# Where ScalarE computes the two magnitudes of a window: the order of ScalarE's instructions in 179 windows of a fused SSM, MLP and FP4 feed-forward kernel

## The chip, the cores and the metric

The kernel runs on one core of a Trainium2 chip. The metric is the device time of one execution in microseconds. The kernel before took 3205.65 us (median of three runs, 3205.09 to 3207.87).

## The reference

The input x is 2 x 4096 tokens of 512 features, in float32. It is layer-normalised to xn, and the output is `x + attn(xn) + ffn(xn)`. The attention branch is a state-space layer and a GELU MLP of width 2048. The feed-forward branch is a gated layer of width 1408 whose operands are all rounded to FP4 in blocks of 16. It is this branch that the change touches:

```python
def fp4_quant_dequant(x):                      # blocks of 16 along the last dim
    xb = x.reshape(shape[:-1] + (shape[-1] // 16, 16))
    scale = max(max|xb| / 6, 1e-12)
    idx = searchsorted(_MID, abs(xb / scale))  # the nearest of 0 .5 1 1.5 2 3 4 6
    return _GRID[idx] * sign(xb) * scale
def fp4_linear(x, w):
    return einsum('bsk,nk->bsn', fp4_quant_dequant(x), fp4_quant_dequant(w))
gate, y = fp4_linear(xn, w_gate), fp4_linear(xn, w_up)
ffn = fp4_linear(silu(gate) * y, w_down)

x1  = xn + ssm_scan(rmsnorm(xn, scale1), A, B, C, D)
attn = x1 + gelu(rmsnorm(x1, scale2) @ w1 + b1) @ w2 + b2
```

## The kernel before

Five engines run programs that are written out by hand and meet at semaphores. After a head (up to 116 us) come 179 windows, numbered by `s`. After them, from 1784 us, the MLP of the attention branch runs alone.

A window works on 256 to 512 tokens and one of 11 slices of 128 hidden features. `h(w)` is the gated product of window w. TensorE computes in window s the gate half and the up half of slice s (L747), and multiplies h(s-2) with the down weights (L769). Each product is done in three passes of a high and a low part, so 12 matmuls each of the three.

All other engines turn h(s-1) into FP4 in that window. In the order of the data:

- ScalarE computes silu(s) from the gate bank into `sg`, L1319. There is one buffer `sg`, so silu(s) also waits until VectorE has taken h(s-1) out of it (L960). TensorE can't begin the gate half of s+1 before silu(s) has read the bank.
- VectorE multiplies (L952), transposes within blocks (L960), and finds the scales (L987, L998, L992). This group is called the front.
- GpSimd divides by the scales, L1518 (`scaled`).
- ScalarE takes absolute values times a constant, L1284 (`magnitude`), into PSUM bank 4, or into `qb` from window 96 on.
- VectorE rounds with two instructions (L1004, L1012), GpSimd multiplies the scales back (L1524, `dequant`), VectorE transposes back (L966).
- In the next window ScalarE rounds to the high part (L1312, `h_high`), and GpSimd subtracts to get the low part (L1532, `h_low`). In GpSimd's program h_low(s-1) stands ahead of scaled(h(s)).

Many windows have a side job as well: in windows 1, 2, 3, 4 and 6 a piece of a weight, in 60 others a tile of 128 tokens of x, to be brought to FP4 in the same way. A side job of window s gets its front and its L1518 at the end of window s, and its rounding in s+1. A weight is then turned by TensorE (L717), split into a high part by ScalarE (L1290, `high`) and a low part by VectorE (L1019, `low`). That is in window s+3, and VectorE's `low` stands ahead of its L960. A tile of x goes out to DRAM and comes back transposed (L508, L516). VectorE takes it up in window s+3 (L1027), and ScalarE makes its high part (L1294).

Further work shares the windows. In windows 11 to 62 it is the SSM's kernel: in 32 windows ScalarE computes two `taps` (an Exp and a Copy each, L1339 and L1347), and two windows after every second of these `kernel_v` (L1355). Exp and Silu have different tables, so each change between them has a table load. In windows 66 to 97 ScalarE writes two tiles of the SSM's input each (`uwrite`, L1371). SyncE sends them to DRAM (L446) four at a time. In windows 99 to 162 the SSM itself runs. ScalarE copies inputs (L1381) in one window and results (L1389) in the next. TensorE has extra matmuls (L793, L810, L818), and VectorE a scan (L1107). Before it can begin, all SSM inputs must be in DRAM: in window 97 GpSimd waits for that (L1589), and SyncE does before it issues the first loads.

In the trace ScalarE's, VectorE's and GpSimd's instructions stand in the order of their programs. So what a `window` function lists first is waited for first. The change touches ScalarE's `window`. On ScalarE `h_job(s)` is h(s-1), `side(s)` the side job of window s.

## Time and profile before

| | |
|---|---|
| three runs | 3205.09, 3205.65, 3207.87 us |
| the profiled execution | 3205.09 us, of which the span of the profile is 3203.3 us |
| TensorE | busy 3081.2 us (96%), granted clock 0.995 |
| VectorE | 2005.0 us (63%) |
| ScalarE | 1090.4 us (34%) |
| GpSimd | 1149.7 us (36%) |
| the chain that ended last | TensorE 60%, VectorE 19%, issue 8%, GpSimd 6%, ScalarE 4% |

A busy share says what an engine does, not what ends last. Matmuls follow each other in a pipeline and their ends are modelled, so TensorE counts as busy where it is near its peak and also where it is a little behind. The pace of the windows shows it better: silu(11) starts at 210.2 us, silu(63) at 661.6, silu(97) at 949.4, silu(103) at 1018.4 and silu(163) at 1652.1.

### The profile page before, as it was taken

How to read it: one execution, taken by the hardware profiler on the slowest of the kernel's cores; microseconds unless marked ns; L12 is line 12 of the kernel's file. 1: busy time of each engine (PE TensorE's matmuls, PEld its weight loads, DVE VectorE, ACT ScalarE, POOL GpSimd, SP SyncE). 2: the span in 40 equal slices, each digit the busy share in tenths (PEclk: the TensorE clock that was granted, in tenths of full speed). 3: DMA queues.
4: the chain of work that ended last, by engine and by line, in shares of the span. 5: the costliest groups of instructions: out<-in, count | busy, mean ns of one | idle time of the engine just before them, and what ended most of it. 6: DMA issues, size and time to landing. Idle time of an engine off the chain costs nothing.

```text
span 3203.3 us, 43122 instructions
## 1 busy us (share of the span) xinstructions
PE 3081.2 (96%) x14861; PEld 2475.4 (77%) x14861; DVE 2005.0 (63%) x4427; ACT 1090.4 (34%) x1910; POOL 1149.7 (36%) x1097
## 2 busy tenths in 40 slices
PE   5789999999998999999999999999999999999999
PEld 3578777777876777777777788888888888888887
DVE  7788888877776666666677654444445444444442
ACT  5435656645443333433332321121222111212121
POOL 7555666655554554554554211010111111111100
PEclk9999999999999999999999999999999999999999
DMA  4133334346765666566643433333333333333320
GB/s 118 47 86 93 109 116 120 85 133 169 188 176 140 161 166 163 143 159 159 159 117 96 124 74 73 73 76 63 79 73 78 68 72 72 73 71 72 74 56 17
DMA packets 865577, 335.58 MB, mean 105 GB/s; under 512 B 680400, under 2 KB 771792, under 8 KB 862800
## 3 DMA queue, kind: packets, MB, share of 16 engines
q1 hardware_dynamic: 865360, 332.83, 42.6%
q8 instruction: 119, 1.95, 0.3%
q14 instruction: 98, 0.80, 0.1%
HBM read 225.21 MB, written 107.51 MB: 104 GB/s over the span
## 4 chain that ended last, share of the span: by engine, by line
PE 60%; DVE 19%; issue 8%; POOL 6%; ACT 4%; SPq 2%; DMA 2%; DVEq 0%; ACTq 0%; POOLq 0%
PE bank L885 22%; PE bank L869 22%; PE bank L747 8%; PE bank L769 4%; POOL qa L1524 3%; DVE qs L987 3%; DVE qa L1004 3%; DVE qa L960 2%; DVE sg L952 2%; DVE qb L1012 2%; POOL qa L1518 2%; PE bank L810 2%; ACT ub L1371 1%; DVE qs L998 1%; DVE qb L966 1%
## 5 line engine op out<-in xcount | busy, mean ns | idle before, releaser
L869 PE MATMUL bank<-hT,Wp 128*128 128x512 f32 x3072 | 745.2, 391 | 4.6 <-ACT gf L1469 2.5
L885 PE MATMUL bank<-Wp,G 128*128 128x512 f32 x3072 | 743.8, 391 | 0.0
L869 PEld LDWEIGHTS bank<-hT,Wp 128*128 128x128 f32 x3072 | 577.7, 188 | 130.7 <-ACT gf L1469 2.9
L885 PEld LDWEIGHTS bank<-Wp,G 128*128 128x128 f32 x3072 | 576.7, 188 | 126.0
L747 PE MATMUL bank<-XT,Wu 128*128 128x512 f32 (+1 forms) x2148 | 520.5, 391 | 28.6 <-DVE sg L952 27.6
L747 PE MATMUL bank<-XT,Wg 128*128 128x512 f32 (+1 forms) x2148 | 525.1, 394 | 18.9 <-DVE Wd L1019 10.2
L769 PE MATMUL bank<-Wd,HT 128*128 128x512 f32 x2112 | 515.0, 392 | 0.5 <-POOL HT L1532 0.3
L747 PEld LDWEIGHTS bank<-XT,Wu 128*128 128x128 f32 x2148 | 397.4, 190 | 132.6 <-issue 53.3
L1218 DVE CAST G<-gf 128x512 fp32r<-128x512 f32 x256 | 110.3, 431 | 610.6 <-PE bank L885 590.1
L747 PEld LDWEIGHTS bank<-XT,Wg 128*128 128x128 f32 x2148 | 398.6, 190 | 108.5 <-issue 15.8
L769 PEld LDWEIGHTS bank<-Wd,HT 128*128 128x128 f32 x2112 | 394.3, 188 | 95.6 <-issue 14.2
L1524 POOL TENSOR_TENSOR qa<-qb,qs 128x512 f32<-128x512 f32 (+2 forms) x277 | 308.0, 1112 | 375.2 <-DVE qb L1012 372.8
L1469 ACT ACTIVATE gf<-bank,vec 128x512 f32<-128x512 f32 x256 | 176.1, 688 | 614.5 <-PE bank L869 614.5
L1518 POOL TENSOR_TENSOR qa<-qa,qs 128x512 f32<-128x512 f32 (+1 forms) x243 | 263.2, 1083 | 225.2 <-DVE qs L992 225.2
L1607 POOL TENSOR_TENSOR zx<-zl,b2r 128x512 f32<-128x512 f32 x64 | 87.0, 1360 | 618.8 <-DMA out_dram<-zx 533.7
L1532 POOL TENSOR_TENSOR HT<-qb,HT 128x512 fp32r<-128x512 f32 (+1 forms) x179 | 230.1, 1286 | 139.3 <-ACT HT L1312 139.2
L1610 POOL TENSOR_TENSOR zx<-zx,xl 128x512 f32<-128x512 f32 x64 | 82.8, 1294 | 515.8 <-DVE xl L1178 515.7
L1312 ACT ACTIVATE HT<-qb 128x512 fp32r<-128x512 f32 (+1 forms) x179 | 112.2, 627 | 351.4 <-DVE qb L966 351.4
L966 DVE STREAM_TRANSPOSE qb<-qa 128x512 f32<-128x512 f32 (+1 forms) x179 | 122.0, 682 | 131.4 <-POOL qa L1524 131.4
L1220 DVE TENSOR_TENSOR G<-gf,G 128x512 fp32r<-128x512 f32 x256 | 185.9, 726 | 8.8
L1319 ACT ACTIVATE sg<-bank 128x512 f32<-128x512 f32 (+1 forms) x179 | 105.8, 591 | 218.4 <-PE bank L747 187.1
L1004 DVE SCALAR_TENSOR_TENSOR qa<-qb,qa 128x512 f32<-128x512 f32 (+2 forms) x149 | 113.2, 760 | 98.4 <-ACT qb L1284 97.9
(114 smaller groups left out, 2840.2 us busy)
## 6 DMA issues: line engine op xcount, KB each, us to landing
px<-in_L_attn_x_dram SPq DMA_DIRECT2D x128, 256.0 KB, 3.2
xin<-in_L_attn_x_dram SPq DMA_DIRECT2D x128, 256.0 KB, 3.5
sT<-r_K SPq DMA_DIRECT2D x128, 256.0 KB, 4.2
r_Z<-xin SPq DMA_DIRECT2D x64, 256.0 KB, 2.2
r_U<-ub SPq DMA_DIRECT2D x16, 1024.0 KB, 6.6
sU<-r_U SPq DMA_DIRECT2D x32, 512.0 KB, 5.2
r_Y<-sY SPq DMA_DIRECT2D x16, 1024.0 KB, 5.7
xl<-in_L_attn_x_dram SPq DMA_DIRECT2D x64, 256.0 KB, 3.1
```

The lines of the kernel that those rows point to most:

```text
L747: ins = e.matmul(bk[:, 0:n], W[wh][:, k, :], inputs(xh, w, k), start=(k == 0 and p_ == 0), stop=(k == KD - 1 and p_ == 2))
L769: ins = e.matmul(DNB[t % 4][:], HT[hh][:, w % 2, a * P:(a + 1) * P], Wd[wh][:, f, :], start=(w == first(n) and p_ == 0), stop=(w == last(n ...
L869: ins = e.matmul(bk[:], Wp[f][wh][:, 0, k * P:(k + 1) * P], hT[xh][b % 2][:, k, :], start=(k == 0 and p_ == 0), stop=(k == KD - 1 and p_ = ...
L885: ins = e.matmul(ACC[j][:], G2[gh][:, n % 2, j * P:(j + 1) * P], Wp[f][wh][:, 1, :], start=(f == 0 and p_ == 0), stop=(f == 15 and p_ == 2))
L966: e.transpose(qb[:, m % 2, 0:n], qa[:, m % 4, 0:n]).then_inc(s_t2, 1)
L1004: e.scalar_tensor_tensor(Aa, Bb, FLOOR, Aa, ALU.max, ALU.add).then_inc(s_t, 1)
L1220: e.tensor_tensor(G2[1][:, n % 2], gf[:, n % 2], G2[0][:, n % 2].bitcast(F32), ALU.subtract).then_inc(s_glo, 1)
L1312: e.activation(HT[0][:, w % 2, 0:n], qb[:, m % 2, 0:n], ACT.Copy).then_inc(s_hh, 1)
L1469: e.activation(gf[:, n % 2], PB[n % 2][:], ACT.Gelu, bias=vec[:, f:f + 1]).then_inc(s_gl, 1)
L1518: e.tensor_tensor(blk(qa[:, m % 4, 0:n]), blk(job_in(m)), bc(qs[:, m % 4, 1, 0:n // 16], n // 16), ALU.mult).then_inc(s_pa, 1)
L1524: e.tensor_tensor(blk(qa[:, m % 4, 0:n]), blk(qb[:, m % 2, 0:n]), bc(qs[:, m % 4, 0, 0:n // 16], n // 16), ALU.mult).then_inc(s_ph, 1)
L1532: e.tensor_tensor(lo, qb[:, m % 2, 0:n], hi.bitcast(F32), ALU.subtract).then_inc(s_hl, 1)
```

## The change

The order of the calls in ScalarE's `window` changes. Nothing is computed in another way, and no other engine's program changes.

- The magnitude of h(s-1) moves from behind silu(s), kernel_v and the uwrites to ahead of silu(s).
- The magnitude of a side job moves from the middle of window s+1 to the end of window s. In the row of ScalarE's instructions it now stands ahead of the next window's `high`, `h_high` and `x_high`, where it was behind them.
- The uwrites move behind the taps; with the magnitude ahead of silu they are also behind that. `kernel_heads` moves ahead of `kernel_v`.

```diff
                 if side(s - 3) in XPOS:
                     x_high(side(s - 3))
-                if side(s - 1) is not None:
-                    magnitude(side(s - 1))
+                if h_job(s) is not None:
+                    magnitude(h_job(s))
                 if s < NW:
                     silu(s)
+                if s in (K0 - 3, K0 - 2):
+                    kernel_heads(s - K0 + 3)
                 if s - 2 in TAPS[1::2]:
                     kernel_v(TAPS.index(s - 2) // 2)
-                for n in plan_slice(s):
-                    if LATER[n][0] == "uw":
-                        uwrite(LATER[n][1])
-                if h_job(s) is not None:
-                    magnitude(h_job(s))
-                if s in (K0 - 3, K0 - 2):
-                    kernel_heads(s - K0 + 3)
                 j = tap_pair(s)
                 if j is not None:
                     kernel_taps(j)
                     kernel_taps(j + 1)
+                for n in plan_slice(s):
+                    if LATER[n][0] == "uw":
+                        uwrite(LATER[n][1])
                 if k == -1:
                     ssm_inputs(0)
                 if 0 <= k < 2 * NV - 2 and k % 2 == 0:
                     ssm_inputs(k // 2 + 1)
+                if side(s) is not None:
+                    magnitude(side(s))
                 if 0 <= k < 2 * NV and k % 2:
                     ssm_result(k // 2)
```

The first place is ScalarE in windows 4 and 5, early in the run, where side jobs are weights. `Wd0<-bank0` is `high`, `HT0<-qb` is `h_high`, `qb<-qa` is the magnitude of the side job and `bank4<-qa` that of h. Before:

```order
L1290 ACTIVATE Wd0<-bank0 128x4x128
L1312 ACTIVATE HT0<-qb 128x256
L1284 ACTIVATE qb<-qa 128x384
L1319 ACTIVATE sg<-bank0 128x512
L1284 ACTIVATE bank4<-qa 128x512
L1290 ACTIVATE Wd0<-bank0 128x3x128
L1312 ACTIVATE HT0<-qb 128x512
```

The same place in the changed kernel:

```order
L1290 ACTIVATE Wd0<-bank0 128x4x128
L1312 ACTIVATE HT0<-qb 128x256
L1284 ACTIVATE bank4<-qa 128x512
L1319 ACTIVATE sg<-bank0 128x512
L1284 ACTIVATE qb<-qa 128x384
L1290 ACTIVATE Wd0<-bank0 128x3x128
L1312 ACTIVATE HT0<-qb 128x512
```

The two magnitudes have changed places around silu. In the second piece the one into `qb` belongs to the next side job, and `high` and `h_high` now stand behind it.

The second place is ScalarE in windows 97 and 98, where the last uwrites are (`ub<-px`). From here the magnitude of h goes into `qb` too. `sUc<-sU` is the first copy of SSM inputs. Before:

```order
L1319 ACTIVATE sg<-bank0 128x512
L1371 ACTIVATE ub<-px,nb,rst 128x32x8 x4
L1284 ACTIVATE qb<-qa 128x512
L1312 ACTIVATE HT0<-qb 128x512
L1284 ACTIVATE qb<-qa 128x512
L1319 ACTIVATE sg<-bank0 128x512
L1284 ACTIVATE qb<-qa 128x512
L1381 ACTIVATE sUc<-sU 128x64x16
```

And in the changed kernel:

```order
L1284 ACTIVATE qb<-qa 128x512
L1319 ACTIVATE sg<-bank0 128x512
L1371 ACTIVATE ub<-px,nb,rst 128x32x8 x4
L1284 ACTIVATE qb<-qa 128x512
L1312 ACTIVATE HT0<-qb 128x512
L1284 ACTIVATE qb<-qa 128x512
L1319 ACTIVATE sg<-bank0 128x512
L1381 ACTIVATE sUc<-sU 128x64x16
```

The four ACTIVATEs of the last uwrites have moved behind the magnitude of h(96) and behind silu(97). The magnitude of side job 97 stands ahead of h_high(96).

## Rows read from the trace of the kernel before

**Rows 1.** Windows view: length; PE, PEld, DVE, ACT, POOL busy; TensorE's clock; DMA; GB/s.

```profile
210.20:661.60 451.40, 440.07 (x1933) 353.39 (x1932) 377.01 (x761) 261.24 (x401) 271.81 (x279) 1.00 0.36 105
...
949.40:1018.40 69.00, 60.71 (x343) 47.04 (x342) 45.92 (x85) 24.84 (x33) 34.35 (x33) 0.95 0.56 136
1018.40:1652.10 633.70, 617.17 (x4081) 482.73 (x4081) 422.77 (x896) 241.60 (x314) 319.25 (x305) 0.99 0.61 157
```

**Rows 2.** Waits of the whole run: us in total, times, longest us.

```profile
DVE qa L1004 <- ACT qb L1284: 97.9, 61, 4.9
```

**Rows 3.** Timeline, windows 79 and 80: start, length, engine and line, idle before.

```profile
798.96 1.06 POOL L1518 TENSOR_TENSOR qa<-qa,qs 128x512 f32<-128x512 f32 x1 [0.76 <-DVE qs L992]
...
800.12 0.58 ACT L1284 ACTIVATE bank<-qa 128x512 f32<-128x512 f32 x1
...
804.02 1.07 POOL L1518 TENSOR_TENSOR qa<-qa,qs 128x512 f32<-128x512 f32 x1 [0.50 <-DVE qs L992]
...
804.55 0.63 ACT L1312 ACTIVATE HT<-qb 128x512 fp32r<-128x512 f32 x1 [3.85 <-DVE qb L966]
...
805.26 1.30 POOL L1532 TENSOR_TENSOR HT<-qb,HT 128x512 fp32r<-128x512 f32 x1 [0.17 <-ACT HT L1312]
...
807.31 1.38 POOL L1518 TENSOR_TENSOR qa<-qa,qs 128x512 f32<-128x512 f32 x1 [0.76 <-DVE qs L992]
```

**Rows 4.** Timeline, window 5 (the weights).

```profile
142.83 0.49 ACT L1290 ACTIVATE Wd<-bank 128x384 fp32r<-128x384 f32 x1 [1.96 <-PE bank L717]
...
145.12 0.84 POOL L1518 TENSOR_TENSOR qa<-xin,qs 128x384 f32<-128x384 f32 x1
...
145.75 0.54 DVE L1019 TENSOR_TENSOR Wd<-bank,Wd 128x384 fp32r<-128x384 f32 x1
...
145.99 0.52 ACT L1284 ACTIVATE qb<-qa 128x384 f32<-128x384 f32 x1
```

**Rows 5.** Timeline, window 9.

```profile
188.90 1.06 POOL L1518 TENSOR_TENSOR qa<-qa,qs 128x512 f32<-128x512 f32 x1 [1.03 <-DVE qs L992]
...
192.50 0.69 DVE L1004 SCALAR_TENSOR_TENSOR qa<-bank,qa 128x512 f32<-128x512 f32 x1 [1.26 <-ACT bank L1284]
```

**Rows 6.** Timeline, window 22 (a table load ahead of silu).

```profile
306.86 1.28 ACT L1319 ACT_TABLE_LOAD   x1
...
308.15 0.60 ACT L1319 ACTIVATE sg<-bank 128x512 f32<-128x512 f32 x1
308.17 1.06 POOL L1518 TENSOR_TENSOR qa<-qa,qs 128x512 f32<-128x512 f32 x1 [1.15 <-DVE qs L992]
...
311.47 3.02 PE L747 MATMUL bank<-XT,Wg 128*128 128x512 f32 x12
```

**Rows 7.** Timeline, windows 97 to 99 (the SSM begins).

```profile
949.90 2.07 ACT L1371 ACTIVATE ub<-px,nb,rst 128x256 f32<-128x256 f32 x4
...
951.99 0.38 SPq L446 DMA_DIRECT2D r_U<-ub  x1
952.13 0.63 ACT L1284 ACTIVATE qb<-qa 128x512 f32<-128x512 f32 x1 [0.16 <-POOL qa L1518]
...
958.38 0.31 POOL L1589 MEMSET sB<- 128x256 f32 x1 [1.95 <-DMA r_U<-ub]
...
976.42 0.71 DVE L1027 STREAM_TRANSPOSE XW<-xin 128x512 f32<-128x512 f32 x1 [8.11 <-DMA xin<-r_X]
...
978.56 4.51 PE L747 MATMUL bank<-XT,Wg 128*128 128x512 f32 x12 [3.81 <-ACT sg L1319]
...
980.22 0.63 ACT L1284 ACTIVATE qb<-qa 128x512 f32<-128x512 f32 x1 [1.80 <-POOL qa L1518]
...
984.91 4.58 PE L747 MATMUL bank<-XT,Wu 128*128 128x512 f32 x12 [1.84 <-DVE sg L952]
```

**Rows 8.** Timeline, windows 126 to 128 (the SSM).

```profile
1262.51 0.32 SPq L508 DMA_DIRECT2D r_X<-qa  x1
...
1285.72 1.98 PE L810 MATMUL bank<-sT,sUc 128*64 128x128 f32 x16 [4.77 <-DVE sS L1107]
```

## The prediction

> **What bounds the kernel now.** I read the windows view first, by stages. In the reader's terms a stage is limited by TensorE where its idle time is near nothing. From 1784 us on that is so, and the change doesn't reach there. In the SSM's stage (windows 103 to 162) TensorE is idle for 633.70 - 617.17 = 16.5 us only; elsewhere it is the bound [rows 1]. In windows 11 to 62 it counts as idle for 451.40 - 440.07 = 11.3 us, and VectorE is busy for 377 of 451 us [rows 1]. There, and in the windows before 11, the timeline shows a ring that no engine can shorten alone: VectorE's product of h, front, GpSimd's L1518, ScalarE's magnitude, VectorE's rounding, GpSimd's L1524, VectorE's transpose back, and then the next product.
>
> Next I read who waits for whom. VectorE waits 97.9 us in 61 cases for the magnitude in `qb` [rows 2]. That looks like the prize of this change. But a wait for an instruction doesn't say that this one was held up by its neighbours. So I compared, window by window, when the magnitude of h starts with when its input is ready. In window 79 GpSimd's L1518 ends at 798.96 + 1.06 = 800.02 and the magnitude starts at 800.12, although the uwrites stand ahead of it [rows 3]. In windows 11 to 97 it is like this nearly everywhere. The wait is the time that GpSimd and ScalarE need. In the SSM's stage the magnitude does stand behind a silu that waits for TensorE's gate half, by 0.4 to 1.4 us, but there TensorE is the bound and VectorE has time.
>
> **What the change costs and gives, stage by stage.** The instructions are the same ones, as many, and as many table loads; only waits move. The h magnitude gets a free way. The price is with what now stands behind a magnitude: in windows after a side job these are `high`, `h_high`, `x_high`, and everywhere silu and the uwrites.
>
> *Windows 1 to 10.* In window s+3 of a weight, VectorE's `low` (L1019) stands ahead of its L960 and waits for ScalarE's `high`. Before, `high` ran as soon as TensorE had turned the weight, at 142.83 for window 5, long before `low` at 145.75 [rows 4]. Now the next side job's magnitude stands ahead of it, and its input is ready at 145.12 + 0.84 = 145.96. So: magnitude until 146.0 + 0.52 = 146.5, `high` until 147.0, `low` at 147.1 instead of 145.75. That is 1.35 us, and it is on the ring: L960, front and everything after move with it. It happens five times, in windows 4, 5, 6, 7 and 9, since the window before each has a side job: 5 x 1.35 = 6.8 us. In three further windows `h_high` alone is late, 0.4 us each by the working of the next paragraph: 1.2 us. Against it stands a gain. In window 9 L1518 ends at 189.96, but VectorE gets the magnitude only for 192.50, after a wait of 1.26 us [rows 5], since silu(9) waits for TensorE. Now it doesn't: -1.2 us, and -0.4 us in two like windows. Together **+6.4 us**. Bounds: +1 if `low` gets room that I don't see (VectorE idle before it; no row shows any), +9 if each is a full magnitude and `high` later than now and nothing is gained.
>
> *Windows 11 to 96.* In window 80 `h_high` ran at 804.55, and `h_low` at 805.26 to 806.56, ahead of L1518 at 807.31 on the same engine [rows 3]. Side job 79's input for its magnitude is ready at 804.02 + 1.07 = 805.09. Now the magnitude comes first, until 805.7, `h_high` until 806.4, `h_low` from 806.4 to 807.7, L1518 at 807.7: 0.4 us late, and the ring with it. Of 13 side jobs in windows 63 to 96, seven lie like this one. At the others VectorE has a tile of x to take up first and hides it. That gives 2.8 us. Of 18 in windows 11 to 62 about eight are not hidden, at 0.4 each, 3.2 us; where there are taps too `h_high` is up to 0.9 us late for L1518, but VectorE has statistics to do there. Gains: the magnitude starts 0.05 us sooner without uwrites ahead of it (some 25 windows), 1.1 us sooner once in window 95, and 0.2 us in four windows with kernel_v: -3 us. Together **+3 us**, with -3 (no `h_high` matters) and +8 (none is hidden) as bounds.
>
> Silu is later as well. In window 22 it ran at 308.15 after its table load; now it must follow L1518 (ends at 309.23), magnitude, load and silu, 0.6 + 1.28 + 0.6, and is over at 311.8. TensorE's next gate half began at 311.47 [rows 6], so it is 0.4 us late, in some ten windows. I cost this at nothing: the up half behind it waits for VectorE's product anyway. If that cover were gone it would be 4 us.
>
> The Trainium skill (ScalarE: Activation LUTs, "What ACT_TABLE_LOAD costs") gives a change of table 1283 ns and a drain of about 1380 ns behind it. The load of 1.28 us is as the page says; the drain is not in this trace, where silu starts at 308.15 and the load ended at 308.14 [rows 6]. By the page silu would be over another 1.4 us later than I have it, and rival 3 is the case that would come of it.
>
> *Windows 97 to 102, where the SSM begins.* The last four ACTIVATEs of the uwrites started at 949.90 and ended at 951.97; the DMA to DRAM was issued at 951.99; and GpSimd could go on at 958.38 after waiting for it [rows 7]. SyncE's first SSM loads wait for the same DMA, and behind them in its queue stands the way back of tile 96, for which VectorE waits 8.11 us until 976.42. Now the uwrites stand behind the magnitude, which can't start before 952.13 and takes 0.63, and behind silu: they start at 953.3, 3.4 us later, and the chain to 976.42 moves with them. A second piece follows. TensorE waited for silu(99) until 978.56. Silu(99) now stands behind a magnitude that starts at 980.22, so it is over at 981.4, and the gate half starts 2.9 us later. It takes 4.51 us at the lower clock, to 986.0; the up half had begun at 984.91, after an idle 1.84. Of the 2.9 us thus 1.1 are left. From here TensorE is the bound. Together 3.4 + 1.1 = **+4.5 us**. Bounds: +1 (the loads hide part of the DMA) and +3.4 + 2.9 = +6.3.
>
> *Windows 103 to 162.* TensorE loses its 16.5 us in eight stalls, the longest 4.77 [rows 1, 8]. They come from tiles of x whose way back is late. The way out is issued when the tile is rounded, as at 1262.51 [rows 8], and VectorE gets there a little earlier now. But SyncE's SSM loads stand in between, and they wait for TensorE's results. I take 0.5 us for each of seven: **-3.5 us**, between 0 and -16.5. In windows where a side magnitude now stands ahead of the copy of results, the copy is about 0.5 us later; it isn't needed before TensorE's next SSM states, most of a window later.
>
> The sum is 6.4 + 3 + 4.5 - 3.5 = +10.4 us. The profiled execution took 3205.09 us, 1.8 more than its span, and stands 0.6 below the median of the runs. So the time is **3215.5 us**, 0.3% slower than before.
>
> **Rivals.**
> 1. *Nothing that can be measured*, 3207 us. Half of the +9.4 us before window 97 is hidden by idle time of VectorE that I don't see, and of the start of the SSM only the 3.4 us stay: 4.7 + 3.4 - 3.5 = 4.6, and another 3 us come back from the stalls in the SSM's stage. For it speaks that VectorE is busy for 377 of 451 us, so it isn't always the one waited for. Against it: the ring waits for one after the other, and idle time of one engine is the work of the next.
> 2. *Faster*, 3197 us. The place is the SSM's stage. If the free magnitude lets each tile of x leave early enough, the eight stalls go, 16.5 us, and with them TensorE's time at the lower clock: the mean of 0.99 [rows 1] over 617 us is some 6 us. That is -22 against +13.9 for the rest. For it: the 97.9 us of waits are mostly in this stage [rows 2]. Against it: it decides from the point at which a tile leaves as much earlier as TensorE's stall lasts, up to 4.8 us, and the magnitude gives 1.4 at most.
> 3. *Much slower*, 3232 us. Silu behind the magnitude holds up TensorE's gate half for so long that the up half and VectorE's next product wait too. The case needs silu to stay away after its table load for about as long again as the load lasts, 1.28 us. Then the gate half is 0.4 + 1.28 = 1.7 us late in some ten windows, 17 us, for TensorE has little room in this stretch. It decides from about 1 us of lateness, the time between the gate half's end and the product that the up half waits for. For it: window 22 has no room left. Against it: the trace shows silu right behind the load [rows 6]. It is what the Trainium skill's rule on the drain would lead to.
>
> **How the numbers follow.** My forecast has a chance of 0.60 (its own range is 3210 to 3224), rival 1 0.23, rival 2 0.09, rival 3 0.08. A difference of 0.2%, 6.4 us, is about what a measurement of this kernel can tell from none. Faster by more than that is rival 2: 0.09. Slower is rival 3 and nine tenths of the forecast, 0.62; the rest, 0.29, is no change. The range that should hold the time 8 times in 10 goes from 3201 (into the ground between rivals 1 and 2) to 3228 us, short of rival 3.
>
> **What would show it.** In window 5 of the changed kernel `low` waits for ScalarE's `high`, by about 1.3 us, where it waited for nothing. In side windows GpSimd's L1532 ends where L1518 begins, without a gap. The DMA r_U<-ub of window 97 is issued about 3.4 us later, after allowing for the shift so far, and the first gate half of the SSM's stage again waits for silu. VectorE's wait for L1284 in the SSM's stage gets shorter and TensorE's stalls hardly do. If silu(11) comes no later than 212 us, the first term is wrong; if silu(103) isn't at least 8 us later than 1018.4, the second and third are; if the stretch from there to silu(163) is shorter by more than 8 us, I misjudged the stalls.

## The result, and the profile after

The changed kernel takes 3249.96 us (median, 3246.31 to 3250.7), the kernel before 3206.76 in the same comparison: ratio 1.0132, interval 1.0114 to 1.0149. The profiled execution of it took 3252.47 us, with a span of 3250.7. The prediction was 3215.5 with a range of 3201 to 3228. The direction was right, and the size was wrong by a factor of four.

Where the time went is best seen by the start of VectorE's L960, which comes once a window. What each stretch takes more than in the kernel before, in us, with the kernels of the experiments below:

| kernel | 1 to 10 | 10 to 62 | 62 to 97 | 97 to 103 | 103 to 163 | 163 to 179 |
|---|---|---|---|---|---|---|
| predicted | +6.4 | +2.4 | +0.4 | +4.5 | -3.5 | 0 |
| changed kernel | +7.4 | +15.0 | +20.6 | +2.9 | -0.9 | +1.7 |
| e1 uwrites first | +7.7 | +15.1 | +6.0 | -1.5 | -0.5 | +1.7 |
| e2 side magnitude in the middle | -0.6 | +3.6 | +12.5 | +1.0 | -0.3 | +1.9 |
| e3 both | -0.7 | +3.6 | -1.8 | -1.7 | -3.5 | +1.9 |
| e4 side magnitude alone | +11.6 | +13.4 | +8.5 | -0.2 | +8.8 | +0.8 |
| e5 uwrites alone | 0.0 | -0.1 | -1.4 | -3.2 | +1.4 | -0.1 |
| e6 scales in PSUM, 66 to 96 | +5.4 | +15.2 | +16.2 | +2.4 | -3.4 | +1.7 |
| e7 `high` first | +0.6 | +15.4 | +18.5 | +2.2 | +1.0 | +1.8 |
| e8 tile out first | +7.5 | +15.3 | +8.4 | +2.7 | -4.5 | +1.8 |
| e9 h first from 64 on | +2.0 | +0.5 | -1.3 | -3.3 | -2.4 | +2.0 |
| e11 scales in PSUM, to 95 | +8.2 | +5.0 | +16.6 | +1.7 | -2.5 | +1.7 |
| e10b e9 with scales in PSUM | +1.9 | -0.5 | +1.4 | -3.4 | -3.0 | +2.0 |

(The prediction's +3 for windows 11 to 96 is 3.2 - 0.8 for its first part, with the gains at kernel_v, and 2.8 - 2.4 for its second.) e5 and e9 have the same program up to window 63 and differ by 2.0 in the first stretch and 0.6 in the second. e7 has the changed kernel's program from window 10 on and differs from it by 0.3 in windows 10 to 62, 2.0 in 62 to 97 (nearly all in window 94) and 1.9 in the SSM's stage, where the five kernels with the changed order (the changed one, e1, e6, e7, e11) lie from -3.4 to +1.0. So fine, and no finer, is what one profile of each tells.

The windows view of the changed kernel, over the windows of [rows 1] (length; PE, PEld, DVE, ACT, POOL busy; clock; DMA; GB/s):

```profile
220.40:687.60 467.20, 442.14 (x1929) 354.91 (x1928) 393.40 (x760) 256.84 (x401) 274.51 (x281) 1.00 0.35 102
996.40:1064.40 68.00, 56.62 (x327) 43.59 (x326) 42.57 (x80) 24.17 (x34) 32.44 (x31) 0.95 0.56 139
1064.40:1699.05 634.65, 617.68 (x4080) 482.95 (x4079) 417.06 (x897) 244.76 (x314) 321.74 (x306) 0.99 0.60 157
```

Windows 11 to 62 are 15.8 us longer, and in them VectorE is busy for 393.40 us instead of 377.01, though it has the same work. Instructions that take longer without doing more are held up inside themselves. That was the first trace of what I had missed. The page of the changed kernel (chain by engine; groups: busy, mean ns, idle before) shows the rest:

```profile
PE 56%; DVE 20%; POOL 8%; issue 8%; ACT 3%; DMA 3%; SPq 2%; DVEq 0%; POOLq 0%; ACTq 0%
...
L1532 POOL TENSOR_TENSOR HT<-qb,HT 128x512 fp32r<-128x512 f32 (+1 forms) x179 | 230.2, 1286 | 241.9 <-ACT HT L1312 241.9
...
L1004 DVE SCALAR_TENSOR_TENSOR qa<-qb,qa 128x512 f32<-128x512 f32 (+2 forms) x149 | 107.2, 719 | 98.6 <-ACT qb L1284 98.4
```

VectorE's wait for the magnitude in `qb`, 97.9 us before [rows 2], is 98.4 us now: the magnitudes came earlier in the program and not earlier for the one who waits. GpSimd's wait for `h_high` went from 139.2 us on the page of before to 241.9.

**Windows 3 to 9.** Window 5 as in [rows 4] (start, length, engine and line, idle before):

```profile
147.24 0.52 ACT L1284 ACTIVATE qb<-qa 128x384 f32<-128x384 f32 x1 [4.02 <-POOL qa L1518]
147.67 0.47 ACT L1290 ACTIVATE Wd<-bank 128x384 fp32r<-128x384 f32 x1
148.04 0.62 ACT L1312 ACTIVATE HT<-qb 128x512 fp32r<-128x512 f32 x1
148.18 0.56 DVE L1019 TENSOR_TENSOR Wd<-bank,Wd 128x384 fp32r<-128x384 f32 x1 [1.10 <-ACT Wd L1290]
148.65 0.70 DVE L960 STREAM_TRANSPOSE qa<-sg 128x512 f32<-128x512 f32 x1
```

Magnitude, `high`, `low`, L960, each on the heels of the one before. `low` waits 1.10 us here and 6.2 us in its five cases. It waited for nothing before.

**Window 80, a side window of x.** Against [rows 3], in the changed kernel:

```profile
834.90 1.06 POOL L1518 TENSOR_TENSOR qa<-qa,qs 128x512 f32<-128x512 f32 x1 [0.51 <-DVE qs L992]
...
836.00 0.63 ACT L1284 ACTIVATE qb<-qa 128x512 f32<-128x512 f32 x1 [1.94 <-POOL qa L1518]
836.07 0.71 DVE L960 STREAM_TRANSPOSE qa<-sg 128x512 f32<-128x512 f32 x1
...
836.53 0.62 ACT L1312 ACTIVATE HT<-qb 128x512 fp32r<-128x512 f32 x1
...
837.23 1.28 POOL L1532 TENSOR_TENSOR HT<-qb,HT 128x512 fp32r<-128x512 f32 x1 [1.26 <-ACT HT L1312]
837.54 1.00 DVE L998 TENSOR_SCALAR qs<-qs 128x32 f32<-128x32 f32 x1
...
839.01 1.38 POOL L1518 TENSOR_TENSOR qa<-qa,qs 128x512 f32<-128x512 f32 x1 [0.51 <-DVE qs L992]
```

The kernel before, VectorE in the same window:

```profile
805.20 0.71 DVE L960 STREAM_TRANSPOSE qa<-sg 128x512 f32<-128x512 f32 x1
...
806.66 0.18 DVE L998 TENSOR_SCALAR qs<-qs 128x32 f32<-128x32 f32 x1
```

ScalarE and GpSimd do what I had worked out: magnitude, `h_high`, `h_low`. But L998, a scaling of 32 columns that took 0.18 us, now takes 1.00 us. It starts at 837.54, while GpSimd's L1532 runs (837.23 to 838.51), and ends at 838.54, when that one is over. From L960 to L1518 it is 839.01 - 836.07 = 2.94 us instead of 807.31 - 805.20 = 2.11: 0.83 us, and the releaser of L1518 is still VectorE's L992 and not L1532. Before, L1532 had ended at 806.56, 0.1 us ahead of L998. Of the window steps (L960 to L960) 7 in windows 11 to 62, 7 in 63 to 96 and 7 in the SSM's stage are longer by 0.80 to 0.84 us, about this number each time.

It is the same wherever L998 is long. All 67 cases over 0.26 us in the changed kernel, and all 38 in the kernel before, end 0.03 to 0.04 us after the end of a GpSimd instruction that ran beside them, L1532 in nearly every case.

**Windows 63 to 97: the late tiles.** Side tile 86 in the changed kernel. (L1371 is the uwrite, L1524 the tile's dequant, L446 the DMA of uwrites, L508 and L516 the tile's way out and back, L1027 its taking up.)

```profile
901.75 2.07 ACT L1371 ACTIVATE ub<-px,nb,rst 128x256 f32<-128x256 f32 x4
```

```profile
901.33 1.07 POOL L1524 TENSOR_TENSOR qa<-qb,qs 128x512 f32<-128x512 f32 x1 [0.63 <-DVE qb L1012]
```

```profile
903.84 0.38 SPq L446 DMA_DIRECT2D r_U<-ub  x1
904.26 4.35 SPq L508 DMA_DIRECT2D r_X<-qa  x1
...
912.29 2.60 SPq L516 DMA_DIRECT2D xin<-r_X  x4
```

```profile
916.65 0.71 DVE L1027 STREAM_TRANSPOSE XW<-xin 128x512 f32<-128x512 f32 x1 [3.18 <-DMA xin<-r_X]
```

The same in the kernel before, SyncE and then VectorE:

```profile
867.34 0.38 SPq L446 DMA_DIRECT2D r_U<-ub  x1
869.16 2.88 SPq L508 DMA_DIRECT2D r_X<-qa  x1
...
875.00 2.60 SPq L516 DMA_DIRECT2D xin<-r_X  x4
...
880.18 0.69 DVE L1027 STREAM_TRANSPOSE XW<-xin 128x512 f32<-128x512 f32 x1
```

The tile was ready at 902.40, when L1524 ended. SyncE stood at L446, which waits for uwrites that end at 903.82; the tile left at 904.26, 1.86 us late. Before, it left 0.02 us after its dequant, at 869.16. It then goes out 0.42 us behind the DMA of uwrites, and I take it that the two share the DMA engines: 8.03 us from the way out to the way back, instead of 5.84. Together 4 us, and VectorE, which had not waited for this tile, waits 3.18. The next such tiles wait 3.17 (0 before) and 4.25 (0.71 before). The steps that answer to them, from windows 88, 92 and 94 to the next, are longer by 3.23, 3.24 and 3.51.

**Windows 97 to 99**, against [rows 7]:

```profile
996.85 2.06 ACT L1371 ACTIVATE ub<-px,nb,rst 128x256 f32<-128x256 f32 x4
...
998.94 0.38 SPq L446 DMA_DIRECT2D r_U<-ub  x1
...
1005.71 0.31 POOL L1589 MEMSET sB<- 128x256 f32 x1 [5.56 <-DMA r_U<-ub]
...
1022.91 0.71 DVE L1027 STREAM_TRANSPOSE XW<-xin 128x512 f32<-128x512 f32 x1 [6.68 <-DMA xin<-r_X]
...
1027.97 3.00 PE L747 MATMUL bank<-XT,Wg 128*128 128x512 f32 x12 [3.38 <-ACT sg L1319]
...
1031.40 2.97 PE L747 MATMUL bank<-XT,Wu 128*128 128x512 f32 x12 [0.43 <-DVE sg L952]
```

L960 of window 97 is at 948.60 before and at 991.47 now. From there the DMA of uwrites is 4.1 us later than before, the tile 3.6 and the gate half 6.5. But the up half is only 3.6 later, since the gate half takes 3.00 us and not 4.51. The windows view of the two gate halves, before and changed, has the reason in its clock column:

```profile
978.50:983.10 4.60, 4.51 (x12) 3.31 (x12) 1.90 (x4) 2.60 (x2) 1.78 (x2) 0.64 0.36 56
```

```profile
1027.90:1031.10 3.20, 3.00 (x12) 2.18 (x12) 1.99 (x4) 2.28 (x2) 2.23 (x2) 1.00 0.07 14
```

TensorE was granted 0.64 of full speed before, a mean of its two levels of 1.2 and 2.4 GHz, and 1.00 now, though its idle time ahead of the gate half is about as long (3.38 us now, 3.81 before). The changed kernel has a longer idle time four groups of products earlier, 5.21 us up to 1010.07, and the 12 matmuls behind that one took 5.49 us.

**The SSM's stage** has its stalls as before. TensorE is idle for 634.65 - 617.68 = 17.0 us in it, where it was 16.5. The longest stall of [rows 8] is still there, 4.24 us instead of 4.77:

```profile
1333.18 1.82 PE L810 MATMUL bank<-sT,sUc 128*64 128x128 f32 x16 [4.24 <-DVE sS L1107]
```

### The profile page after: what moved, and what is told of

Read it like the earlier page. It is cut to its first block, busy times and chain, and to the rows that moved or that the text cites. A ratio compares the mean times of both kernels' runs of the same rounds, so it can differ in the third digit from the quotient of the medians.

```text
span 3250.7 us, 43122 instructions
## 1 busy us (share of the span) xinstructions
PE 3094.8 (95%) x14861; PEld 2480.5 (76%) x14861; DVE 2025.7 (62%) x4427; ACT 1085.2 (33%) x1910; POOL 1152.3 (35%) x1097
## 4 chain that ended last, share of the span: by engine, by line
PE 56%; DVE 20%; POOL 8%; issue 8%; ACT 3%; DMA 3%; SPq 2%; DVEq 0%; POOLq 0%; ACTq 0%
PE bank L885 21%; PE bank L869 21%; PE bank L747 7%; POOL qa L1524 3%; DVE qs L987 3%; POOL qa L1518 3%; PE bank L769 3%; DVE qa L1004 3%; DVE qa L960 2%; DVE qb L1012 2%; DVE sg L952 2%; DVE qs L998 2%; DMA r_X<-qa 1%; PE bank L810 1%; DVE qs L992 1%
## 5 line engine op out<-in xcount | busy, mean ns | idle before, releaser
L747 PE MATMUL bank<-XT,Wg 128*128 128x512 f32 (+1 forms) x2148 | 533.2, 398 | 33.9 <-ACT sg L1319 19.2
L1524 POOL TENSOR_TENSOR qa<-qb,qs 128x512 f32<-128x512 f32 (+2 forms) x277 | 308.9, 1116 | 324.4 <-DVE qb L1012 321.9
L1518 POOL TENSOR_TENSOR qa<-qa,qs 128x512 f32<-128x512 f32 (+1 forms) x243 | 261.7, 1077 | 213.2 <-DVE qs L992 213.2
L1532 POOL TENSOR_TENSOR HT<-qb,HT 128x512 fp32r<-128x512 f32 (+1 forms) x179 | 230.2, 1286 | 241.9 <-ACT HT L1312 241.9
L1284 ACT ACTIVATE qb<-qa 128x512 f32<-128x512 f32 (+2 forms) x149 | 93.1, 625 | 390.6 <-POOL qa L1518 390.3
L987 DVE TENSOR_REDUCE qs<-qa 128x32 f32<-128x512 f32 (+1 forms) x243 | 165.2, 680 | 8.4
L1004 DVE SCALAR_TENSOR_TENSOR qa<-qb,qa 128x512 f32<-128x512 f32 (+2 forms) x149 | 107.2, 719 | 98.6 <-ACT qb L1284 98.4
```

Source lines behind the costliest of these rows:

```text
L747: ins = e.matmul(bk[:, 0:n], W[wh][:, k, :], inputs(xh, w, k), start=(k == 0 and p_ == 0), stop=(k == KD - 1 and p_ == 2))
L987: e.tensor_reduce(s_, blk(job_in(m)), AX, ALU.max, apply_absolute_value=True).then_inc(s_mx, 1)
L1004: e.scalar_tensor_tensor(Aa, Bb, FLOOR, Aa, ALU.max, ALU.add).then_inc(s_t, 1)
L1518: e.tensor_tensor(blk(qa[:, m % 4, 0:n]), blk(job_in(m)), bc(qs[:, m % 4, 1, 0:n // 16], n // 16), ALU.mult).then_inc(s_pa, 1)
L1524: e.tensor_tensor(blk(qa[:, m % 4, 0:n]), blk(qb[:, m % 2, 0:n]), bc(qs[:, m % 4, 0, 0:n // 16], n // 16), ALU.mult).then_inc(s_ph, 1)
L1532: e.tensor_tensor(lo, qb[:, m % 2, 0:n], hi.bitcast(F32), ALU.subtract).then_inc(s_hl, 1)
```

## The experiments

e1, e2, e6, e7, e8 and e11 alter the changed kernel; e3, e4, e5, e9 and e10b alter the kernel before. All ratios are to the kernel before, which took 3207 to 3210 us beside them. They are close to the quotients of the medians, not equal to them.

### e1 to e4: which of the moves

ScalarE's window in short, where `uw` are the uwrites and `res` the SSM's results:

```
before:  x_high, side(s-1), silu, kernel_v, uw, h, heads, taps, inputs,             res
changed: x_high,            h, silu, heads, kernel_v, taps, uw, inputs, side(s),    res
e1:      x_high, uw,        h, silu, heads, kernel_v, taps,     inputs, side(s),    res
e2:      x_high, side(s-1), h, silu, heads, kernel_v, taps, uw, inputs,             res
e3:      x_high, side(s-1), uw, h, silu, heads, kernel_v, taps, inputs,             res
e4:      x_high,            silu, kernel_v, uw, h, heads, taps, inputs, side(s),    res
```

> The changed kernel, with the uwrites alone put back ahead of the magnitude of h (and so ahead of silu). Theory A, two causes: the uwrites behind silu hold SyncE's queue, so that tiles of x leave late for DRAM (steps of 2.4, 2.2, 3.2, 3.2 and 3.5 us at windows 70, 76, 88, 92 and 94, and 2.8 at 98, 17 us in all); the rest is the side magnitude ahead of h_high. It expects 3250 - 17 = 3233 us, and none of these steps. Rival B: the loss comes from silu behind the magnitude of h, which is still so here; then 3247 us or more.

Measured: 3235.31 us, ratio 1.0077 (1.0062 to 1.0092). The late uwrites cost 14.6 us in windows 62 to 97 and 4.4 us at the SSM's start, and nothing elsewhere. Window 94 has 3.5 of the 14.6; in e2, e6, e7 and e11, where the uwrites are as late, it has 1.6 to 1.7, so that 12.7 us may be nearer. The steps of 2.2 to 3.5 us in windows 70, 76, 88, 92 and 94 are gone, and those of 0.83 are left, in 64, 65, 69, 75, 76, 80, 86 and 91.

> The changed kernel, with the magnitude of a side job alone put back behind h_high and x_high of the next window. Theory A: the side magnitude ahead of h_high costs 7.3 us in windows 1 to 10 and 0.83 us in some 30 side windows after that, 25 us; without it 3250 - 32 = 3218 us, and the time of VectorE's L998 that is over its own length falls from 40.7 us to about the 18.6 of before. Rival B (silu behind the magnitude of h): above 3240 us.

Measured: 3223.49 us, ratio 1.0039 (1.0024 to 1.0054), 5 us more than expected. The weights' +7.4 is gone. None of the 21 windows that were longer by 0.80 to 0.84 us is so now. What is left in windows 62 to 97 is the late uwrites.

> Both put back: the order is h_high, x_high, side magnitude, uwrites, magnitude of h, silu, taps. Of the change only the magnitude of h ahead of silu is left, and the uwrites stand even earlier than before. Theory A: no loss is left and the gains remain (window 9, window 95, tiles of x and the SSM's first loads leave earlier): 3198 to 3203 us. Rival B: what is left is its cause, so 3215 us or more.

Measured: 3205.16 us, ratio 0.9979 (0.997 to 0.9989), 2 us above the range of 3198 to 3203 that was expected, and far below rival B's 3215. With both put back, only the magnitude of h ahead of silu remains of the change (and the uwrites ahead of silu). It gains 1.7 to 3.5 us in each of three stretches and loses 3.6 in windows 10 to 62.

> The kernel before, with one part of the change alone: the magnitude of a side job at the end of its window. Theory A: 3206 + 32 = 3238 us. Rival B expects no more than 3212 us, since silu stands as before.

Measured: 3246.69 us, ratio 1.0109 (1.0089 to 1.0129), 9 us more than expected. The move of the side magnitude, alone, makes nearly the whole loss. In the SSM's stage it costs 8.8 us where the changed kernel doesn't lose. Eight windows there are longer by 0.83 to 0.88, as window 108 of e4:

```profile
1105.40 1.30 POOL L1532 TENSOR_TENSOR HT<-qb,HT 128x512 fp32r<-128x512 f32 x1 [1.26 <-ACT HT L1312]
1105.71 1.03 DVE L998 TENSOR_SCALAR qs<-qs 128x32 f32<-128x32 f32 x1
```

It is the pair of window 80, in seven of the eight. But this doesn't add up to the 8.8 us: summed over the stage, what the long cases of L998 take over 0.18 us is 7.6 us in e4 and 8.7 in the kernel before, since in other windows it is now held up less. TensorE stands idle for 23.8 us in the stage instead of 16.5, all but a little of it ahead of L810. What brings these stalls isn't shown. In the changed kernel seven of the eight windows are just as long, and yet the stage isn't longer than in e2 and e3 (-0.3 and -3.5), which have the side magnitude in the middle. So with the magnitude of h ahead of silu, the move of the side magnitude costs this stage nothing that the profiles tell. The 11.6 us in windows 1 to 10, against 7.4 in the changed kernel, lie in two steps, windows 4 (2.61, 1.11 in the changed kernel) and 6 (2.79, 1.48); what ends last there I haven't followed.

### e5: the uwrites ahead of silu, in the kernel before

```diff
+                for n in plan_slice(s):
+                    if LATER[n][0] == "uw":
+                        uwrite(LATER[n][1])
                 if s < NW:
                     silu(s)
```

> The kernel before, with the uwrites alone moved, ahead of silu. Nothing of the change is in it. Theory A: tiles of x and the SSM's inputs leave earlier, so the SSM's stage begins 2 to 3 us earlier; 3206 us against 3209 of the kernel before. If the magnitude of h ahead of silu is what gives the gain of the run with both put back, this one is within 0.5 us of the kernel before.

Measured: 3208.08 us beside 3209.86, ratio 0.9995 (0.9986 to 1.0003): no change that can be told. The profile shows -3.2 us at the SSM's start and +1.4 in its stage. By the ratios the larger part of e3's gain would be the magnitude of h and not this (0.9979 against 0.9995), but the two intervals touch, and in the profiles e5 is 3.4 us shorter than the kernel before and e3 2.2. It isn't shown.

### e6 and e11: is it L998 that waits for GpSimd?

The block maxima (L987) go to PSUM, so that L998 has one operand there and one in SBUF. e6 does this for h in windows 66 to 96 (bank 7), e11 for all jobs up to window 95 (bank 4, as shown; `rounded` counts the jobs that VectorE has rounded so far, since those read the bank too).

```diff
-                biggest(m)
+                if m < MSSM - 1:
+                    p_ = bank[4][:, 0:job_width(m) // 16]
+                    if rounded[0]:
+                        e.wait_ge(s_q, rounded[0])
+                biggest(m, p_)
                 e.wait_ge(s_mx, m + 1)
-                e.tensor_scalar(s_, s_, 1.0 / 6.0, 1e-12, ALU.mult, ALU.max)
+                e.tensor_scalar(s_, p_, 1.0 / 6.0, 1e-12, ALU.mult, ALU.max)
```

> The changed kernel; in windows 66 to 96 VectorE's L987 writes the block maxima of h to a free PSUM bank, and L998 reads them there and not in SBUF. Theory C: of the 0.83 us per side window 0.4 is GpSimd's L1532 standing longer ahead of L1518, and 0.43 is that L998 can't run beside L1532 when it reads and writes SBUF, so that it takes 1.0 us instead of 0.18; with a PSUM operand it is free. Then L998 takes 0.2 us in windows 69, 75, 80, 86 and 91, and these steps shrink from 0.83 to about 0.4 us. Rival D: L998 is late for another reason (the chain through the scales, or ScalarE); then the steps stay at 0.83 and L998 at 1.0 us.

Measured: 3242.38 us, one time (3207.17 for the kernel before). L998 took 191 to 193 ns in all 31 windows. Windows 69, 75, 80, 86 and 91 are longer by 0.41 or 0.42 instead of 0.83; windows 64 and 65, where nothing was altered, still by 0.83.

> The changed kernel, with one difference in all fronts up to window 95, not only in those of 66 to 96 as before: L987 writes the block maxima to PSUM bank 4, and VectorE's first scaling (L998) reads them there and writes to SBUF. In the changed kernel L998 took 15.9 us over its own time in windows 11 to 62 and 8.8 us in 63 to 97. Theory P (L998 with both operands in SBUF can't run beside GpSimd's L1532): each L998 takes 0.19 us, and as in the earlier experiment about half of the excess comes back, since L992 and what follows still meet GpSimd: windows 11 to 62 lose about 7 to 8 us against the kernel before instead of 15.0, windows 63 to 97 about 16, the whole is about 3239 us. Theory R (in windows 11 to 62 the loss is silu, taps and table loads standing behind late instructions, and L998 only fills time that is waited for anyway): windows 11 to 62 still lose 13 us or more, the whole is 3244 us or more.

Measured: 3237.12 us, ratio 1.0092 (1.0076 to 1.0107). Windows 10 to 62 lose 5.0 us instead of 15.0, windows 62 to 97 16.6 instead of 20.6. No step of 0.83 is left in windows 11 to 96. Every L998 of this stretch has its own time (a line's view: count, then min, median, max ns):

```profile
L1005 DVE TENSOR_SCALAR qs<-bank x133: 174/191/194, 118.2 to 953.1; 128x32 f32<-128x32 f32 x126, 128x24 f32<-128x24 f32 x4, 128x16 f32<-128x16 f32 x3
L1005 DVE TENSOR_SCALAR qs<-qs x111: 174/182/1114, 963.7 to 1820.1; 128x32 f32<-128x32 f32 x108, 128x16 f32<-128x16 f32 x3
```

and window 80 now is what the prediction took it for (L1540 is L1532 here, L1005 L998, L1526 L1518):

```profile
825.70 0.71 DVE L960 STREAM_TRANSPOSE qa<-sg 128x512 f32<-128x512 f32 x1
...
826.86 1.28 POOL L1540 TENSOR_TENSOR HT<-qb,HT 128x512 fp32r<-128x512 f32 x1 [1.26 <-ACT HT L1320]
827.23 0.19 DVE L1005 TENSOR_SCALAR qs<-bank 128x32 f32<-128x32 f32 x1
...
828.10 1.51 POOL L1526 TENSOR_TENSOR qa<-qa,qs 128x512 f32<-128x512 f32 x1
```

The scaling runs in 0.19 us in the middle of GpSimd's instruction, and L1518 starts right when L1532 ends. The window is 0.42 us longer than before, the 0.4 of the prediction. With both operands in SBUF it is 0.83.

### e7: `high` ahead of the side magnitude

```diff
                 if side(s - 3) in TPOS:
                     high(side(s - 3))
+                    if side(s - 1) is not None:
+                        magnitude(side(s - 1))
...
-                if side(s) is not None:
+                if side(s) is not None and side(s - 2) not in TPOS:
                     magnitude(side(s))
```

> The changed kernel; in the windows where a weight's high part is due, the side magnitude stands behind it and not ahead of it, still ahead of h_high. The theory of the prediction: VectorE's low (L1019) waits for high, five times about 1.35 us, 6.8 of the 7.4 us that windows 1 to 10 lose. It expects that stretch to lose 2 us at most over the kernel before. Rival E: h_high and the port are the cause there as elsewhere; then 5 us or more stay.

Measured: 3244.39 us, one time. Windows 1 to 10 lose 0.6 us instead of 7.4, and no `low` waits:

```profile
141.94 0.49 ACT L1290 ACTIVATE Wd<-bank 128x384 fp32r<-128x384 f32 x1 [1.94 <-PE bank L717]
...
144.86 0.54 DVE L1019 TENSOR_TENSOR Wd<-bank,Wd 128x384 fp32r<-128x384 f32 x1
```

### e8: the tile leaves ahead of the uwrites, on SyncE

```diff
+                if side(s - 1) in XPOS:
+                    tile_out(side(s - 1))
                 for n in plan_slice(s):
                     px_load(LOADAT[LATER[n]] + 3)
                     if LATER[n][0] == "uw":
                         u_out(LATER[n][1])
-                if side(s - 1) in XPOS:
-                    tile_out(side(s - 1))
```

> The changed kernel; on SyncE alone, the DMA that sends a tile of x out (L508) is issued ahead of the window's px loads and the SSM inputs' way out, which wait for the uwrites. The uwrites stay late on ScalarE. Theory A: the steps at windows 70, 76, 88, 92 and 94 (14.6 us) come from tiles that leave late because SyncE waits for uwrites; so they go, and the kernel takes about 3237 us, with the 2.8 us at window 98 still there. Rival F: the late uwrites hurt by themselves (ScalarE is late for h_high, or the DMAs of the SSM's inputs collide with the tiles'); then it stays at 3247 us or more.

Measured: 3238.87 us, ratio 1.0101 (1.0084 to 1.0117). ScalarE's order is the changed one, with its late uwrites. Windows 62 to 97 lose 8.4 us instead of 20.6. Tile 86, SyncE and VectorE:

```profile
898.77 0.33 SPq L508 DMA_DIRECT2D r_X<-qa  x1
900.20 0.38 SPq L446 DMA_DIRECT2D r_U<-ub  x1
905.91 3.22 SPq L516 DMA_DIRECT2D xin<-r_X  x4
...
911.00 0.71 DVE L1027 STREAM_TRANSPOSE XW<-xin 128x512 f32<-128x512 f32 x1 [1.16 <-DMA xin<-r_X]
```

The tile no longer stands behind L446, and VectorE waits 1.16 us for it, not 3.18. That it is late at all I put down to the traffic of the uwrites, which wasn't tested apart: 7.14 us from the way out to the way back, 5.84 before.

### e9 and e10b: the magnitude of h ahead of silu in a part of the windows

e9 is e3 with the magnitude of h ahead of silu in windows 64 to 162 alone, and behind kernel_v elsewhere as before.

```diff
-                if h_job(s) is not None:
+                if h_job(s) is not None and 64 <= s < 163:
                     magnitude(h_job(s))
                 if s < NW:
                     silu(s)
...
+                if h_job(s) is not None and not 64 <= s < 163:
+                    magnitude(h_job(s))
```

> The order of the run with both put back, but with the magnitude of h ahead of silu in windows 64 to 162 only. That run lost 3.6 us in windows 10 to 62 and 1.9 us in the last 16 over the kernel before, and gained 7 us elsewhere. Theory A expects both losses to go: 5 us below that run, 8 us below the kernel before (0.997 of its time at most). If the losses don't belong to silu behind the magnitude, it is as fast as that run, 0.998.

Measured: 3204.06 us beside 3209.86, ratio 0.9981 (0.9972 to 0.9989). The loss of windows 10 to 62 is gone (+0.5). The 1.9 us of the last 16 windows, which theory A expected to go too, are still there (+2.0). It isn't told apart from e3 by its time, where 5 us less were expected; both are faster than the kernel before by about 0.2%.

> The order of e9 (side magnitude in the middle as before, uwrites ahead of silu, the magnitude of h ahead of silu only in windows 64 to 162) and the block maxima in PSUM for all fronts up to window 95. There L998 took 1.9 + 5.8 + 0.7 = 8.4 us over its own time in windows 1 to 97. Theory P: half of that comes back, 4 us: 3200 us beside 3204 for e9, ratio to the kernel before about 0.9965. Theory R: what L998 waited for was hidden: 3204 us, ratio 0.998.

Measured: 3206.46 us beside 3209.22, ratio 0.9992 (0.9983 to 1.0). Nothing was gained in sum: windows 10 to 62 are 1.1 us shorter than in e9, and windows 62 to 97 2.7 longer. Window by window there are two parts. From window 11 on, L998 took 0.48 us or more in eleven windows of e9. Ten of them (14, 17, 19, 28, 30, 39, 41, 50, 61 and 63) are shorter by 0.23 to 0.59 us, 4.1 us together, which is what theory P expected; window 52 isn't. Most others are longer by 0.05 to 0.14 us. That is a toll of the edit: the 48 maxima of windows 62 to 97 were preceded by 4.1 us of idle time instead of 1.7, and the maxima in bank 4 have one wait more.

e11 has the same toll, and it too is freed of waits that the kernel before had. So L998's share in the loss is read from e11 against e10b, not against the changed kernel. In windows 10 to 62, where e10b has ScalarE's order of the kernel before, e11 takes 5.6 us more than e10b, and the changed kernel takes 15.0 more than the kernel before: 9.4 us hang on L998. In windows 62 to 97, with window 94 left out, e11 takes 14.3 us more than e10b and the changed kernel 18.3 more than e9: 4.0 us.

## Why the prediction was wrong, step by step

**Windows 1 to 10: right.** +6.4 predicted, +7.4 measured (5.4 to 7.7 in e1, e6 and e8, which have the same order there), and e7 takes 6.8 of it back. `low` waited 6.2 us in five cases (6.8 predicted), behind magnitude and `high` as worked out from [rows 4]. That the sum comes so near is in part luck: the five windows cost 8.3 us, and the gain of 1.2 us in window 9 was 0.2 in this profile (1.3 in e1 and e6).

**Windows 11 to 96: +3 predicted, +35.6 measured. This is the step that failed**, by four faults. The count of the side windows that aren't hidden was right (seven of 13, and seven where about eight of 18 were forecast); their price wasn't.

- *The size of one unhidden side window, 0.4 us.* The mechanism was right, since it is what e11 shows. Missing was a second one on top: L998 takes 1.00 us instead of 0.18 when GpSimd's L1532 runs beside it. Before, `h_low` ended 0.1 us ahead of L998; the change moved it right onto it. That L998 stalls was to be seen in the trace of before: 38 of its 244 cases exceed 0.26 us, the longest 1.24. In the changed kernel 67 do, and what these take over 0.18 us each is 42.5 us in all, where it was 18.7. The Trainium skill (SBUF — State Buffer, "SBUF: two separate sides") calls the port pair that GpSimd and VectorE share "an exclusive lock, not a bandwidth split", and has it taken by a VectorE operation in a two-port mode; VectorE: DVE Perf Modes ("What auto-detection actually checks") has this mode for one source and a destination both in SBUF. L998 was such an operation. e6 and e11 agree with both pages: with the source in PSUM it took 0.19 us or less in all of its 31 and 133 cases.
- *The cover of windows with taps.* I wrote that `h_high` may be 0.9 us late there because VectorE has statistics to do. In windows 14, 21, 32, 43 and 54 this cost 0.50 to 0.69 us each, about 3 us, in the changed kernel and in e11, and nothing in e3. The ring goes through GpSimd's L1518, and statistics on another engine don't cover that.
- *SyncE's queue.* I counted what stands behind the uwrites on ScalarE and not who waits for them. That was SyncE at L446, with a tile of x behind it in its queue. I had followed that chain in window 97 and in no other. Moving the tile ahead (e8) gives back 12.2 of the 20.6 us, moving the uwrites (e1) 14.6. I had even put earlier starts "without uwrites ahead" among the gains.
- *Silu, and with it the taps, behind the magnitude.* I asked only what TensorE loses by a late silu. The taps stand behind silu, and the next window's `h_high` behind the taps. This is 3.3 of the 3.6 us that e3 loses in windows 10 to 62, and in the changed kernel 2.3 us, in windows 33, 37 and 55, which e4 leaves alone. It is worked out below.

With the shares as measured, windows 10 to 62 are 9.4 us L998 and 5.6 the rest (e11 against e10b): about 3 in the five windows with taps, 1.5 in the seven side windows, 1.0 in window 55. Windows 62 to 97 are 14.6 us late uwrites (e1) and 4.0 us L998, which leaves 2.0 us; the prediction had 2.8 for the side windows there, less 1.1 for window 95, which came (1.07).

**Silu behind the magnitude costs nothing: right for TensorE, wrong for the ring.** In window 22 TensorE's gate half begins 7.6 us after L960, instead of 5.4, a good deal later than I had it (0.4), because kernel_v too stands behind silu and TensorE's L780 waits for it. Yet this window is only 0.36 us longer, and not at all in e11. Rival 3 is therefore refuted by its own place, though the measured time lies 18 us above its 3232. Silu follows its table load at once in the changed kernel too:

```profile
321.29 1.28 ACT L1319 ACT_TABLE_LOAD   x1
...
322.58 0.60 ACT L1319 ACTIVATE sg<-bank 128x512 f32<-128x512 f32 x1
```

What silu behind the magnitude does cost is in windows 27, 33, 37 and 55. e3 loses 1.13, 0.57, 0.54 and 1.06 us in them, 3.3 of its 3.6, and e9, with the old order there, nothing. In the window ahead of each, the taps run behind a silu that has become late, and `h_high` stands behind the taps. In window 55 of the kernel before it starts 1.08 us ahead of L960; in e3 it starts 0.65 us behind it. Then GpSimd's `h_low` runs beside L998, which takes 1.25 us. But it costs as much where L998 doesn't wait. In e11 window 55 is 1.02 us longer with L998 at 0.19 us, because L1518 now comes behind `h_low` (the last tap, `h_high`, `h_low`, L1518; L960 is at 604.51, and L1518 started 2.07 us after it in the kernel before):

```profile
605.37 0.40 ACT L1355 ACTIVATE kC<-kE,ks 128x128 f32<-128x128 f32 x1
605.68 0.61 ACT L1320 ACTIVATE HT<-qb 128x512 fp32r<-128x512 f32 x1
...
606.37 1.29 POOL L1540 TENSOR_TENSOR HT<-qb,HT 128x512 fp32r<-128x512 f32 x1 [2.70 <-ACT HT L1320]
...
607.61 1.06 POOL L1526 TENSOR_TENSOR qa<-qa,qs 128x512 f32<-128x512 f32 x1
```

**The SSM's start: +4.5 predicted, +2.9 measured.** The chain through the last uwrites came out as worked out (tile 3.6 us later, 3.4 predicted; gate half 6.5, 6.3 predicted). The 1.1 us of the gate half were wrong, since it ran at a clock of 1.00 and not at the 0.64 of before. I had carried the duration of one clock to another situation.

**The SSM's stage: -3.5 predicted, -0.9 measured.** With -3.4 to +1.0 in the profiles of the same order, the two are hardly told apart. I gave the side magnitude no cost here, "TensorE is the bound". e4 shows +8.8 for it, but only with silu ahead of the magnitude of h, and how it comes about is open. The stalls stayed, as rival 2 needed them not to. VectorE's wait for L1284 in this stage was 78.8 us and is 76.4.

**Windows 163 to 179: 0 predicted, +1.7 measured.** It comes in every kernel that has the magnitude of h ahead of silu in the SSM's stage, in e9 too, which has the old order from 163 on; so it is brought along from there: it lies in the step of window 163 (1.98 us in e3). Its cause is open.

**The signs that the prediction named.** `low` waits (1.10 us in window 5, 1.3 forecast), the DMA of the last uwrites is 4.1 us later (3.4), the first gate half of the SSM's stage waits for silu. One sign was missed and would have told the fault at once: L1532 was to end where L1518 begins, but between 838.51 and 839.01 there is a gap of 0.5 us, in which VectorE's L992 comes late. The thresholds all asked whether a term was too large (silu(11) came at 220.4, silu(103) at 1064.4). None asked whether one was too small, and the bound of +8 for windows 11 to 96 came from the same 0.4 us that was wrong (31 side jobs at 0.4 less the 3 of gains are even 9.4).

## What to carry to other kernels

Before an instruction is delayed on one engine, list everything that waits for it, on DMA queues too, and all that stands behind those waiters: here SyncE stood at one DMA for uwrites, and a tile that had nothing to do with them left 1.86 us late. When GpSimd's work is moved in time, look at what VectorE does at the new time, and not only at who waits for whom; lone long cases of a short VectorE instruction (0.18 us at the median, 1.24 at most) that end with a GpSimd instruction are the mark of it in the trace of before. And a wait of 98 us on the page for an instruction is no prize, if this one starts 0.1 us after its own input.

## What the runs showed of the hardware

- A VectorE instruction of 32 columns, SBUF to SBUF, takes 1.00 to 1.03 us instead of 0.18 when it starts 0.3 us into a GpSimd instruction of 1.28 to 1.30 us, and ends 0.04 us after that one. With its source in PSUM it takes 0.19 us at the same place. The 0.69 us reduction ahead of it, which reads 512 columns and writes 32, was not held up.
- TensorE's gate half after 3.38 us without work ran at the full clock (1.00, 3.00 us), and after 3.81 us in the kernel before at 0.64 (4.51 us). Right before the idle time both did three groups of 12 matmuls (the kernel before with 1.25 us idle among them) and the same 16 small ones (L793). Further back they differ: the changed kernel had 5.21 us without work, after which 12 matmuls took 5.49 us.
- A tile's way out and back took 8.03 us behind a DMA of uwrites issued 0.42 us ahead of it, 7.14 with that DMA issued 1.43 us behind it, and 5.84 with it issued 1.82 us ahead.
